# Order of TensorE's products in three attention layers: whole-array products together, scores next to shift, the output product a step later, the output bias on GpSimd

## The chip, the cores and the metric

The kernel runs on one core of a Trainium2 chip. The metric is the time of one execution in device microseconds; the median of several runs is compared. Five engines work side by side: TensorE (PE; its weight loads are shown as PEld), VectorE (DVE), ScalarE (ACT), GpSimd (POOL) and SyncE (SP), which starts transfers. Each takes its own instructions in order and waits for semaphores that others raise. TensorE writes to PSUM, in eight banks; VectorE and ScalarE read it from there.

## The reference

Eight blocks follow each other on x of 16 sequences, 128 tokens, 256 channels. Four are attention blocks on a context, each followed by a feed-forward block. The change touches the attention of the second, third and fourth pair, which compute this (the second with a window, the fourth with rotary embeddings):

```python
q = (Q @ Wq.T + bq).reshape(B, Lq, H, DH).transpose(0, 2, 1, 3)
k = (K @ Wk.T + bk).reshape(B, Lk, H, DH).transpose(0, 2, 1, 3)
v = (V @ Wv.T + bv).reshape(B, Lk, H, DH).transpose(0, 2, 1, 3)
scores = jnp.einsum('bhlp,bhmp->bhlm', q, k) / math.sqrt(DH)
attn = jax.nn.softmax(scores, axis=-1)
out = jnp.einsum('bhlm,bhmp->bhlp', attn, v)
out = out.transpose(0, 2, 1, 3).reshape(B, Lq, D)
return out @ Wo.T + bo          # x = x + this, of layernorm(x) and the context
```

There are 16 heads of 16 channels.

## The kernel before

`attention(nc, env, layer, windowed, rotary)` is called three times: windowed (layer 1), full (layer 2), rotary (layer 3). It holds all 16 sequences in SBUF. A first stage projects keys, values and queries and turns the normalised x (`xn`, made by VectorE, in the rotary layer by ScalarE). Then a loop of steps follows, one sequence n entering at each, with the work on a sequence spread over several steps. Every engine has its own copy of the loop, and the order within a step is written out by hand: the order in which TensorE's, ScalarE's and VectorE's queues hold their instructions.

The stages of sequence n, in order of the data:

- `maxima(n)` on TensorE: f16 products of all heads, 16 instructions on 32-row tiles of the array; in the windowed layer `add_window` precedes it with eight 64x64 products (line 812). VectorE's `maxima(n, 0)` and `(n, 1)` (line 1149) reduce them, half each, to `neg_max`, of which there is one buffer: they wait for `max_turned`, that `turn_maxima(n - 1)` has read it.
- `turn_maxima(n)` (line 838): one whole-array transpose of `neg_max`; ScalarE's `maxima_out(n)` (line 1010) copies it to `neg_maxT`.
- `scores(n)` (line 851): f32 products on 32-row tiles; they wait for ScalarE's exponentials of n - 1 and for the first reduction of n + 1, whose banks they overwrite. `shift(n)` (line 862) adds `neg_maxT` in the same banks.
- ScalarE's `exponentials(n, 0)` and `(n, 1)` (line 1016). The products of `maxima(n + 2)` wait for the first of them.
- `weigh_values(n)` (line 874): 32 products on 32-column tiles, after both exponentials and after `normalise(n - 1)` has read the bank; ScalarE's `sums_out(n)` (line 1028) copies the result.
- `turn_sums(n)` (line 881): four whole-array transposes; VectorE's `normalise(n)` (lines 1155 and 1158): reciprocal and product, to `att`.
- `turn_attended(n)` (line 888): two whole-array transposes; ScalarE's `attended_out(n)` (line 1023).
- `output(n)` (line 895): four whole-array products; VectorE's `add_output(n)` (line 1164) adds them to X, `restate(n)` (line 100) takes the statistics of X for the next block.

`add_bias(n)` on VectorE (line 1102) adds the output bias to X. `hold_clock` (line 55) gives TensorE whole-array products whose result nobody reads. `normal_ahead` is a chain of small VectorE instructions that prepares the next block's normalisation from the statistics of the first 12 sequences.

TensorE's step n before is: turn_maxima(n), maxima(n + 1), turn_sums(n - 2), output(n - 3), scores(n), turn_attended(n - 2), shift(n), weigh_values(n - 1). VectorE's step n: maxima(n + 1, 0), add_bias(n), normalise(n - 2), add_output(n - 3), maxima(n + 1, 1), restate(n - 3).

## Time and profile before

| | us |
|---|---|
| median of 3 runs (2058.22 to 2061.71) | 2058.24 |
| the profiled execution | 2056.44 |
| its span in the trace | 2054.1 |
| PE busy in the span | 1817.9 (88%) |
| DVE busy | 1519.5 (74%) |
| ACT busy | 1133.2 (55%) |
| POOL busy | 158.7 (8%) |

How to read the rows below. A row of the timeline has the start in us from the start of the span, the time from the first start to the last end in us, the engine, the line of the kernel, the operation, the tile written and the tiles read, their shapes, how many instructions are merged in it, and in square brackets how long the engine stood idle before it and what ended that. Ends of matmuls are modelled. A row of the view of one line has the engine, the operation, the count, the least, median and greatest duration in ns, and the first and last start in us. A row of the windows table has the stretch, its length, then for PE, PEld, DVE, ACT and POOL the busy time with the number of instructions, the granted clock of TensorE as a share of full speed, the share of DMA, and GB/s.

### The profile page before, as it was taken

How to read it: one execution, taken by the hardware profiler on the slowest of the kernel's cores; microseconds unless marked ns; L12 is line 12 of the kernel's file. 1: busy time of each engine (PE TensorE's matmuls, PEld its weight loads, DVE VectorE, ACT ScalarE, POOL GpSimd, SP SyncE). 2: the span in 40 equal slices, each digit the busy share in tenths (PEclk: the TensorE clock that was granted, in tenths of full speed). 3: DMA queues.
4: the chain of work that ended last, by engine and by line, in shares of the span. 5: the costliest groups of instructions: out<-in, count | busy, mean ns of one | idle time of the engine just before them, and what ended most of it. 6: DMA issues, size and time to landing. Idle time of an engine off the chain costs nothing. (4 is left out here: it accounts for less than half of the span.)

```text
span 2054.1 us, 40735 instructions
## 1 busy us (share of the span) xinstructions
PE 1817.9 (88%) x16084; PEld 1324.4 (64%) x16084; DVE 1519.5 (74%) x3172; ACT 1133.2 (55%) x1916; POOL 158.7 (8%) x129
## 2 busy tenths in 40 slices
PE   7959258997799999999999999988997897799994
PEld 6844155665466666666666666655674466688884
DVE  6987886667777777777777776787766777688886
ACT  3535754556366666666666665526542654467762
POOL 0001300000000000000000000000000100244431
PEclk9979689998999999999999999999999998799997
DMA  6120001003000000000000000010001001577775
GB/s 222 47 79 0 0 1 52 2 3 114 21 22 22 22 21 22 22 22 22 23 24 24 15 1 1 1 53 2 3 21 56 1 3 46 187 255 245 248 258 173
DMA packets 80365, 120.90 MB, mean 59 GB/s; under 512 B 9840, under 2 KB 62512, under 8 KB 80048
## 3 DMA queue, kind: packets, MB, share of 16 engines
q1 hardware_dynamic: 75760, 106.22, 15.6%
q0 software_dynamic: 4416, 12.06, 1.7%
q8 instruction: 130, 2.13, 0.4%
q14 instruction: 59, 0.48, 0.1%
HBM read 103.58 MB, written 14.68 MB: 58 GB/s over the span
## 5 line engine op out<-in xcount | busy, mean ns | idle before, releaser
L2586 PE MATMUL sl_ps_eo<-sl_w,sl_hT 128*128 128x256 f16 x3072 | 353.2, 273 | 0.8 <-DVE sl_hT L2829 0.7
L2563 PE MATMUL sl_ps_h<-sl_slot_inT,sl_w 128*128 128x512 f16 x1536 | 338.3, 379 | 0.5 <-ACT sl_h L2706 0.5
L2586 PEld LDWEIGHTS sl_ps_eo<-sl_w,sl_hT 128*128 128x128 f16 x3072 | 298.5, 98 | 35.8 <-DVE sl_hT L2829 1.3
L2706 ACT ACTIVATE sl_h<-sl_ps_h,sl_b1T 128x512 f32<-128x512 f32 x256 | 175.6, 687 | 170.3 <-PE sl_ps_h L2563 163.3
L2563 PEld LDWEIGHTS sl_ps_h<-sl_slot_inT,sl_w 128*128 128x128 f16 x1536 | 149.9, 98 | 176.3 <-ACT sl_h L2706 2.4
L2829 DVE TENSOR_TENSOR sl_hT<-sl_h,sl_hT 128x512 f16<-128x512 f32 x256 | 176.8, 692 | 102.2 <-ACT sl_hT L2709 97.9
L1149 DVE TENSOR_REDUCE at_neg_max<-at_ps 128x8 bf16<-128x1024 f32 x96 | 116.9, 1220 | 68.2 <-PE at_ps L831 68.2
L2125 PE MATMUL mo_ps_h<-mo_xgT,mo_w 128*128 128x256 f16 x1104 | 125.9, 275 | 3.5 <-issue 2.1
L2843 DVE SCALAR_TENSOR_TENSOR sl_result<-sl_ps_eo,sl_b 128x256 f32<-128x256 f32 x128 | 54.3, 424 | 97.8 <-PE sl_ps_eo L2586 93.5
L2136 PE MATMUL mo_ps_eo<-mo_w,mo_hT 128*128 128x256 f16 x1104 | 124.1, 273 | 0.0
L2125 PEld LDWEIGHTS mo_ps_h<-mo_xgT,mo_w 128*128 128x128 f16 x1104 | 108.1, 99 | 19.0 <-issue 5.8
L2136 PEld LDWEIGHTS mo_ps_eo<-mo_w,mo_hT 128*128 128x128 f16 x1104 | 107.1, 98 | 12.0
L1016 ACT ACTIVATE at_probT<-at_ps 128x1024 f32<-128x1024 f32 x96 | 98.6, 1027 | 15.0 <-PE at_ps L862 15.0
L2188 ACT ACTIVATE mo_h<-mo_ps_h,mo_b 128x256 f32<-128x256 f32 x184 | 77.0, 475 | 46.6 <-issue 42.8
L1224 POOL MEMSET at_v<- 128x2048 f32 x6 | 10.7, 1816 | 1122.5 <-POOLq L85 1122.5
L2709 ACT ACTIVATE sl_hT<-sl_h 128x512 f16<-128x512 f32 x128 | 80.6, 629 | 4.0
L1023 ACT ACTIVATE at_attT<-at_ps 128x256 f32<-128x256 f32 x48 | 18.4, 383 | 109.9 <-PE at_ps L888 109.9
L2685 ACT ACTIVATE sl_combT<-sl_ps_lt 128x512 f32<-128x512 f32 x32 | 19.1, 597 | 108.5 <-PE sl_ps_lt L2542 108.5
L1615 PE MATMUL qf_ps<-qf_xqT,qf_w_inT 128*128 128x512 f16 x288 | 66.5, 393 | 8.3 <-DVE qf_xqT L1814 6.0
L2317 DVE SCALAR_TENSOR_TENSOR mo_w<-mo_w_raw,mo_w 128x1024 f16<-128x1024 f32 x46 | 56.2, 1223 | 23.9 <-ACT mo_w L2170 23.9
L2208 POOL DMA_INDIRECT mo_xg<-x_rows,mo_from_i x46 | 60.7, 1320 | 146.3 <-DVE mo_from_i L2299 131.3
L2170 ACT ACTIVATE mo_w<-mo_w_raw 128x1024 f16<-128x1024 f32 x46 | 48.5, 1056 | 38.9 <-DMA mo_w_raw<-in_L_ffn_W 38.9
(435 smaller groups left out, 3629.8 us busy)
## 6 DMA issues: line engine op xcount, KB each, us to landing
mo_w_raw<-in_L_ffn_W SPq DMA_DIRECT2D x46, 1024.0 KB, 8.7
sl_w_in<-in_L_ffn_w SPq DMA_DIRECT2D x16, 1024.0 KB, 5.4
at_ctxT<-ctx_pairs SPq DMA_DIRECT2D x9, 512.0 KB, 7.3
mo_w_raw<-pair_rows SPq DMA_DIRECT2D x4, 1024.0 KB, 9.0
mo_b<-in_L_ffn_b SPq DMA_DIRECT2D x23, 128.0 KB, 4.9
ac_attention_w<-L_attention_w SPq DMA_DIRECT2D x3, 768.0 KB, 12.4
w_pairs<-ac_w_pair SPq DMA_DIRECT2D x3, 768.0 KB, 3.2
ac_ctx_all<-in_ctx SPq DMA_DIRECT2D x4, 512.0 KB, 8.2
```

The costliest lines, as they stand in the source:

```text
L1016: act.activation(probT[:, n % 2, 2 * pair:2 * pair + 2].rearrange("p r j q -> p r (j q)"), ps[:, at:at + 2], ACT.Exp, scale=SCALE).then_in ...
L1149: dve.tensor_reduce(neg_max[:, 2 * pair:2 * pair + 2, 0:HR], ps[:, at:at + 2].rearrange("p r (j k) -> p r j k", j=HR), AX.X, ALU.max, nega ...
L1615: last = pe.matmul(pair(q)[:, g], w_inT[:, w, i, k, c * P:(c + 1) * P], xqT[:, x, k, tokens], start=(k, a) == (0, 0), stop=(k, a) == (C - ...
L2125: last = pe.matmul(ps_h[:, q % 3, j % 2], w1_of(m, wp)[:, k, j * P:(j + 1) * P], xgT[:, m % 2, xp, k], start=(k, a) == (0, 0), stop=(k, a) ...
L2136: last = pe.matmul(ps_eo[:, s, 0:D], hT[:, m % 2, hp, j, s * P:(s + 1) * P], w2_of(m, wp)[:, j], start=(j, a) == (0, 0), stop=(j, a) == (H ...
L2188: act.activation(h[:, q % 2, j % 2], ps_h[:, q % 3, j % 2], ACT.Relu, bias=b1[:, m % WB, j:j + 1], scale=1.0 / W_SCALE).then_inc(h_ready, 1)
L2208: pool.indirect_dma_start(xg[:, m % XB, s], None, env.x_rows, bass.IndirectOffsetOnAxis(ap=from_i[:, q:q + 1].bitcast(U32), axis=0)).then_ ...
L2563: last = pe.matmul(ps_h[:, j % 2], w1[:, e % 2, w, k, j * P:(j + 1) * P], slot_inT[:, q % 2, x, k].rearrange("p b s -> p (b s)"), start=(k ...
L2586: last = pe.matmul(ps_eo[:, b % 2, 0:D], hT[:, hp, j, b * P:(b + 1) * P], w2[:, e % 2, w, j], start=(j, a) == (0, 0), stop=(j, a) == (HJ - ...
L2706: act.activation(h[:, j % 2], ps_h[:, j % 2], ACT.Gelu, bias=b1T[:, q // G4, j:j + 1], scale=1.0 / W_SCALE).then_inc(h_ready, 1)
L2709: act.activation(hT[:, 0, j], h[:, j % 2], ACT.Copy).then_inc(h_high, 1)
L2829: dve.tensor_tensor(hT[:, 1, j], h[:, j % 2], hT[:, 0, j], ALU.subtract).then_inc(h_split, 1)
```

## The change

TensorE's step n becomes: weigh_values(n - 2), maxima(n + 1), turn_attended(n - 3), turn_sums(n - 2), turn_maxima(n), output(n - 4), scores(n), shift(n); turn_maxima(0) stands ahead of the loop, and there is one more step. VectorE does both reductions first, then normalise(n - 2), add_output(n - 4) and restate(n - 4); normal_ahead comes a step later. ScalarE's loop is put in the order that fits. The transposed maxima move from bank 7 to columns of bank 6 that nobody reads between the turned sums, and the waits for who uses which bank are changed with it. The bias additions move from VectorE's steps to GpSimd, each as soon as `xn` of its sequence is made; in the rotary layer they stand ahead of GpSimd's casts.

```diff
+UNREAD = DH + 4
...
-        ps_max = ps_a[:, 0, 0:P // 2].bitcast(BF16)
+        ps_max = ps[:, 6].bitcast(BF16).rearrange("p (k i) -> p k i", i=2 * 32)[:, :, 2 * UNREAD:2 * UNREAD + P // H]
...
             def turn_maxima(n):
                 pe.wait_ge(max_ready, 2 * n + 2)
-                enough(pe, attT_ready, n - 2)
...
                 enough(pe, att_ready, n)
+                pe.wait_ge(maxT_ready, min(n + 2, B))
...
             def turn_attended(n):
                 pe.wait_ge(att_ready, n + 1)
-                enough(pe, out_added, n)
+                enough(pe, attT_ready, n)
+                enough(pe, out_added, n - 1)
...
             def output(n):
                 pe.wait_ge(attT_ready, n + 1)
-                pe.wait_ge(maxT_ready, min(n + 4, B))
+                enough(pe, out_added, n)
...
-            for n in range(B + 3):
-                if n < B:
-                    turn_maxima(n)
-                if n == 1:
-                    hold_clock(pe, env, ps[:, 6, 0:P], 2)
+            turn_maxima(0)
+            for n in range(B + 4):
+                if 2 <= n < B + 2:
+                    weigh_values(n - 2)
                 if n + 1 < B:
                     maxima(n + 1)
+                if n < 3:
+                    hold_clock(pe, env, ps[:, 7, 0:P], 4)
+                if 3 <= n < B + 3:
+                    turn_attended(n - 3)
                 if 2 <= n < B + 2:
                     turn_sums(n - 2)
-                if n >= 3:
-                    output(n - 3)
-                if n < 2:
-                    hold_clock(pe, env, ps[:, 6, 0:P], 4)
+                if 1 <= n < B:
+                    turn_maxima(n)
+                if n >= 4:
+                    output(n - 4)
                 if n < B:
                     scores(n)
-                if 2 <= n < B + 2:
-                    turn_attended(n - 2)
-                if n < B:
                     shift(n)
-                if 1 <= n <= B:
-                    weigh_values(n - 1)
...
-            for n in range(B + 2):
-                if n >= 2:
-                    attended_out(n - 2)
+            for n in range(1, B + 3):
+                if n <= B:
+                    exponentials(n - 1, 0)
+                if 2 <= n < B + 2:
+                    sums_out(n - 2)
+                if n <= B:
+                    exponentials(n - 1, 1)
                 if n < B:
-                    exponentials(n, 0)
-                if 1 <= n <= B:
-                    sums_out(n - 1)
-                if n + 1 < B:
-                    maxima_out(n + 1)
-                if n < B:
-                    exponentials(n, 1)
+                    maxima_out(n)
+                if n >= 3:
+                    attended_out(n - 3)
...
             def normalise(n):
                 link = Links(dve, att_link, 1, n)
                 dve.wait_ge(sums_turned, n + 1)
+                dve.wait_ge(maxT_ready, min(n + 3, B))
...
             def add_output(n):
                 dve.wait_ge(out_made, n + 1)
+                dve.wait_ge(attT_ready, min(n + 2, B))
...
-            for n in range(B + 3):
+            for n in range(B + 4):
                 if n + 1 < B:
                     maxima(n + 1, 0)
-                if n < B:
-                    add_bias(n)
+                    maxima(n + 1, 1)
                 if 2 <= n < B + 2:
                     normalise(n - 2)
-                if n >= 3:
-                    add_output(n - 3)
-                if n + 1 < B:
-                    maxima(n + 1, 1)
-                if n == AHEAD + 3:
+                if n >= 4:
+                    add_output(n - 4)
+                if n == AHEAD + 4:
                     normal_ahead(dve, t, env, 1, restated, AHEAD, rows_only=windowed)
-                if n >= 3:
-                    restate(n - 3)
+                if n >= 4:
+                    restate(n - 4)
...
+            pool.wait_ge(consts_in, CONSTS)
+            for n in range(B):
+                pool.wait_ge(t.xn_ready, n + 1)
+                pool.tensor_tensor(t.X[:, n], t.X[:, n], bo[:], ALU.add).then_inc(bo_added, 1)
```

## Rows read from the trace of the kernel before

**Rows 1.** Windows table: most steps of the rotary layer; the full layer's tail.
```profile
1634.00:1706.00 72.00, 68.45 (x1271) 47.45 (x1270) 54.52 (x108) 42.41 (x69) 0.00 (x0) 1.00 0.01 3
...
1480.00:1492.00 12.00, 8.71 (x120) 6.10 (x112) 6.83 (x31) 4.25 (x7) 0.00 (x0) 1.00 0.00 0
```

**Rows 2.** Timeline of the rotary layer, one step, from scores to scores.
```profile
1664.18 0.25 DVE L1155 RECIPROCAL at_inv_sum<-at_ps 128x16 f32<-128x16 f32 x1
...
1664.21 1.15 PE L851 MATMUL at_ps<-at_QT,at_KT 32*128 32x256 f32 x16
1664.46 0.42 DVE L1158 TENSOR_TENSOR at_att<-at_ps,at_inv_sum 128x256 f32<-128x256 f32 x1
1664.81 0.41 DVE L1164 TENSOR_TENSOR X<-X,at_ps 128x256 f32<-128x256 f32 x1
...
1665.36 0.41 PE L888 MATMUL at_ps<-early_ident,at_att 128*128 128x128 f32 x2
...
1665.70 0.40 PE L862 MATMUL at_ps<-at_neg_maxT,at_slot_sel 32*128 32x128 bf16 x16
...
1666.04 1.08 PE L874 MATMUL at_ps<-at_probT,at_v 128*32 128x128 f32 x32
1666.16 1.02 ACT L1016 ACTIVATE at_probT<-at_ps 128x1024 f32<-128x1024 f32 x1
...
1667.05 0.23 PE L838 MATMUL at_ps<-at_ident_b,at_neg_max 128*128 128x128 bf16 x1
...
1667.83 0.42 PEld L881 LDWEIGHTS at_ps<-early_ident,at_sumsT 128*128 128x128 f32 x4 [0.28 <-ACT at_sumsT L1028]
...
1668.33 1.03 PE L895 MATMUL at_ps<-at_wo,at_attT 128*128 128x256 f32 x4
...
1669.29 1.15 PE L851 MATMUL at_ps<-at_QT,at_KT 32*128 32x256 f32 x16
```

**Rows 3.** Timeline of the windowed layer, its first two steps.
```profile
367.63 1.02 ACT L1016 ACTIVATE at_probT<-at_ps 128x1024 f32<-128x1024 f32 x1 [2.57 <-PE at_ps L862]
...
368.80 0.62 PE L812 MATMUL at_ps<-at_window_b,at_ident_b 64*64 64x256 bf16 x8 [0.55 <-ACT at_probT L1016]
...
369.81 1.22 DVE L1149 TENSOR_REDUCE at_neg_max<-at_ps 128x8 bf16<-128x1024 f32 x1 [2.74 <-PE at_ps L831]
...
371.18 0.62 PE L812 MATMUL at_ps<-at_window_b,at_ident_b 64*64 64x256 bf16 x8 [0.34 <-DVE at_neg_max L1149]
...
371.74 1.15 PE L851 MATMUL at_ps<-at_QT,at_KT 32*128 32x256 f32 x16
...
373.03 1.08 PE L874 MATMUL at_ps<-at_probT,at_v 128*32 128x128 f32 x32
```

**Rows 4.** Timeline of the windowed layer, a later step: maxima, then turn_sums.
```profile
404.90 0.40 PE L831 MATMUL at_ps<-at_ctxT,at_QT_half 32*128 32x128 f16 x16
...
405.23 0.66 PE L881 MATMUL at_ps<-early_ident,at_sumsT 128*128 128x128 f32 x4
```

**Rows 5.** View of line 862 (shift): the windowed layer, then the rotary layer.
```profile
L862 PE MATMUL at_ps<-at_neg_maxT,at_slot_sel x256: 214/214/225, 367.2 to 456.5; 32*128 32x128 bf16 x128
...
L862 PE MATMUL at_ps<-at_neg_maxT,at_slot_sel x256: 214/214/226, 1631.1 to 1706.4; 32*128 32x128 bf16 x128
```

**Rows 6.** Timeline of VectorE at the windowed layer's end: normal_ahead to statistics; last statistics.
```profile
454.79 0.90 DVE L143 BATCH_NORM_AGGREGATE ahead_meanvar<-stats 128x2 f32<-128x6 f32 x12
...
458.39 0.43 DVE L100 BATCH_NORM_STATS2 stats<-X 128x6 f32<-128x256 f32 x1
...
467.37 0.43 DVE L100 BATCH_NORM_STATS2 stats<-X 128x6 f32<-128x256 f32 x1
```

**Rows 7.** Timeline of the rotary layer's projections: a GpSimd cast beside VectorE.
```profile
1607.84 1.04 POOL L1229 CAST at_QT_half<-at_QT 128x1024 f16<-128x1024 f32 x1 [50.64 <-ACT at_QT L987]
1607.86 1.56 DVE L1118 TENSOR_TENSOR at_q_turned<-at_by_cos,at_by_sin 128x512 f32<-128x512 f32 x1
```

**Rows 8.** View of line 1110: by_sin, whose one input is in PSUM.
```profile
L1110 DVE TENSOR_TENSOR at_by_sin<-at_ps,at_sinT x16: 678/682/691, 1563.8 to 1624.2; 128x512 f32<-128x512 f32 x16
```

More of the change, by code:

```diff
@@ L1009, in maxima_out @@
                 enough(act, shifted, n)
-                act.activation(neg_maxT[:], ps_max, ACT.Copy).then_inc(maxT_ready, 1)
+                act.activation(neg_maxT[:].rearrange("p (k i) -> p k i", i=P // H), ps_max, ACT.Copy).then_inc(maxT_ready, 1)
             def exponentials(n, pair):
@@ L1099, in normal_x @@
                                   ALU.subtract, ALU.mult).then_inc(t.xn_ready, 1)
-            def add_bias(n):
-                dve.tensor_tensor(t.X[:, n], t.X[:, n], bo[:], ALU.add).then_inc(bo_added, 1)
             def rope(job, to, wait_for, ready):
```

## Prediction

> **What bounds the kernel now.** The change touches only the three attention layers, so I read the windows table first: in the 72 us that hold most steps of the rotary layer TensorE is busy 68.45 us at a granted clock of 1.00 (the 2.4 GHz level), VectorE 54.52 and ScalarE 42.41 [rows 1]. A step is a TensorE queue that hardly stops. The timeline of one rotary step shows its links; from the scores of one step to those of the next are 5.08 us [rows 2]. The gaps of TensorE are turns between array shapes. The scores, with turn_attended between them and shift, reach weigh_values after 1.83 us [rows 2]; where the first steps have no turn_attended, the same stretch takes 1.29 [rows 3]. That half microsecond is what the new order goes for. Nothing else of the three layers is slack in this sense: VectorE spends two reductions of 1.22 [rows 3], a reciprocal, a product, an addition and the statistics on each step, which fit beside TensorE only because the first reduction may start early.
>
> I take links as distances between starts. An instruction's consumer on another engine starts 0.06 after its written end (shift 1665.70 + 0.40, exponential 1666.16 [rows 2]), and one that follows on the same VectorE starts 0.07 before it (attended product to addition, 0.35 for 0.42 [rows 2]).
>
> **What the change removes, on TensorE alone.** Scores and shift together: 1.83 becomes 1.29, minus 0.54. turn_maxima loses its own turn of shapes and turn_attended too, but both stay as work: four whole-array transposes take 0.49 to 0.50 from turn_sums to output [rows 2], so 0.12 each, and 0.24 for the two of turn_attended. A step of TensorE's own pieces in the new order would be: scores to weigh_values 1.29, weigh_values to the next shape 1.01 (to turn_maxima [rows 2]), maxima 0.33 [rows 4], attended 0.24, sums 0.49, maxima's transpose 0.12, output 0.96 [rows 2]: 4.44 against 5.08. The rule behind this is in the Trainium skill, TensorEngine Tiling (Array Packing), section Key Properties: changing the tiling mode, not just the tile, drains TensorE. The trace agrees (1.83 against 1.29); by that rule alone the three layers would gain, which is the first rival below.
>
> **What the new order ties together.** neg_max has one buffer, so VectorE's maxima(n + 1) waits until turn_maxima(n) has read it; this wait is not touched by the diff. Before, turn_maxima(n) opened step n, ahead of the products of maxima(n + 1), and the wait was long over. Now it stands behind maxima(n + 1), turn_attended(n - 3) and turn_sums(n - 2), and turn_sums waits for ScalarE's sums_out, which waits for weigh_values. Behind the waiting reduction stand, on VectorE, the second reduction, normalise(n - 2), add_output and restate; and weigh_values(n - 1) waits for normalise(n - 2). That closes a loop through three engines, which I walk for the layers without a window:
> weigh_values to turn_sums 1.79, ended by ScalarE's copy (1666.04 to 1667.83 [rows 2]; the products of maxima and turn_attended, 1.01 + 0.33 + 0.24 = 1.58, are hidden in it); turn_sums to turn_maxima 0.49; its end and the reaction 0.23 + 0.06 = 0.29; two reductions at 1.22 - 0.07 = 1.15, 2.30, both now ahead of normalise; reciprocal to product 0.28; product to weigh_values 0.55, as from add_output to turn_attended (1664.81 to 1665.36 [rows 2]). Sum 5.70 against 5.08.
> Scores in this loop: they wait for the first reduction, 1.37 after its start [rows 3], so they start 1.79 + 0.49 + 0.29 + 1.37 = 3.94 behind weigh_values, 0.95 later shift, and weigh_values follows at 5.70, not at 5.23: normalise comes last.
>
> In the windowed layer the window's products (0.56 from their start to the scores [rows 3]; taken as the same ahead of maxima) come twice a step, and another loop is longer. From turn_maxima: 0.29 to the reduction, 1.37 to the window's products of the scores, 0.56 to the scores. The next maxima have to wait for the first exponential: scores to shift 1.29 - 0.34 = 0.95, shift to exponential 0.46, exponential to the window's products 1.17 (367.63 to 368.80 [rows 3]), 2.58 together, more than the 1.29 + 1.01 that TensorE needs; before, turn_maxima stood in this place. Then 0.56 to maxima, 0.33, 0.24, 0.49 to turn_maxima. Sum 6.42. The VectorE loop is shorter here: 1.01 + 0.56 + 0.33 + 0.24 + 0.49 + 0.29 + 2.30 + 0.28 + 0.55 = 6.05.
>
> **Sum of the steps.** From shift(0) to shift(15) there are 15 distances. The first two have the four clock-holding products in them (eight whole-array instructions at 0.12, 0.97). Without a window: exponential 0.46, maxima 1.17 later, 0.33, 0.97, 0.29, 1.37, 0.95: 5.54; the next with turn_sums 0.49 more, 6.03; twelve of 5.70, 68.4; the last has no reduction to wait for: 0.81 (5.70 - 3.94 - 0.95) + 1.79 + 0.49 + 0.12 + 0.96 + 0.95 = 5.12. Total 85.1. The trace has 1706.4 - 1631.1 - 0.2 = 75.1 in the rotary layer (the row's last start is the last of one shift's sixteen products, so 0.2 comes off) [rows 5], and the full layer repeats its pattern, so twice +10.0. With the window: 6.66 + 7.15 + 12 x 6.42 + 5.2 = 96.0 against 456.5 - 367.2 - 0.2 = 89.1 [rows 5], +6.9.
>
> **The end of a layer.** There is one more step, but the tail's links (attended, output, addition) are those of before. What moves is normal_ahead: it now stands in step 16 ahead of normalise(15), 3.6 us of VectorE (454.79 to 458.39 [rows 6]) in a tail of 467.37 - 456.3 = 11 us, where it used to lie a step before normalise(14) and was over when turn_sums(14) came. Bounds: nothing, if the chain outlasts it, and the whole 3.6. Counted from shift(15), turn_sums(14) comes at 0.34 + 1.79 = 2.13, weigh_values(15) at 2.13 + 0.71 + 0.28 + 0.55 = 3.67 and turn_sums(15) at 5.46, so normalise(15) could begin at 6.2. VectorE's addition behind output(12) ends at some 4.4, and with 3.6 and the statistics it is free at 8.4. I take 2.0 for each layer, 6.0.
>
> **Edits costed at nothing, and their cover.** add_bias leaves VectorE: 16 additions a layer that lay in VectorE's waits; it would help only if the reductions did not wait. weigh_values' wait for maxima_out is for the step before. normalise's wait for maxima_out(n) is covered by two reductions, 2.3 us, in which ScalarE ends at most one exponential (1.02 [rows 3]) and a short copy. add_output's wait for attended_out has output's 1 us before it and the reductions beside it. Scores keep their waits. SP has no new DMA. Without these covers each would cost its own copy, under 0.4.
>
> **GpSimd's additions.** The trace has no such instruction of GpSimd; they run in the projections, as each xn is ready, and ahead of the rotary layer's casts in its queue. What they can do is seen beside those casts: a 1.04 us cast started at 1607.84, and the VectorE product of two SBUF tiles at 1607.86 took 1.56 instead of 0.69 [rows 7]; by_sin, with one input in PSUM, stayed between 678 and 691 ns in all 16 [rows 8]. In the other two layers VectorE has no instruction with two SBUF tiles between the first xn and the last, so the lower bound there is zero; none reaches below zero but what add_bias gave back, already counted. In the rotary layer at most one such instruction falls into a group of four: 4 x 0.87 = 3.5. I take zero, nearest to the by_sin row, and keep 3.5 for the range. The Trainium skill, SBUF — State Buffer, section Who interferes with whom, says that a VectorE instruction with two SBUF inputs contends with a GpSimd instruction that reads SBUF and that whoever is second is blocked. The 1.56 agrees; the sum is the same by it.
>
> **Result.** 10.0 + 10.0 + 6.9 + 6.0 = 32.9. The profiled execution took 2056.44 (span 2054.1), so 2089.3; the median of the three runs, 2058.24, is 0.1% above it, and there it is 2091. Error of the walk: the links not seen in this order are product to weigh_values (0.49 to 0.66), turn_sums to turn_maxima (0.39 to 0.55), attended to sums (0.12 to 0.34) and weigh_values to the next shape (0.9 to 1.1): about -0.25 and +0.3 for each of 36 steady steps, -9 and +11. With the tail (-6 to +5) not all one way, 2077 to 2106.
>
> **Rivals.**
> 1. Faster: the shapes decide, as the rule on draining would have it. The place is the start of the first reduction: if it followed the products of maxima and not turn_maxima, the loop would fall below TensorE's own sum. It decides once the reduction starts 0.62 earlier than in my walk without a window, 0.42 with it. Without the wait a step is 2.58 + 0.33 + 0.24 + 0.49 + 0.12 + 0.96 = 4.72 and with the window 5.84; over 30 and 15 steps minus 13, plus 6 for the tails: 2051. For it: the 0.54. Against it: one buffer, and a reduction would overwrite what is still to be read.
> 2. No change: the loops close, but my links are too long by half a microsecond each step, as if the transposes came with less than half of their cost and turn_sums did not wait: 2055 to 2062.
> 3. Slower still by the clock: TensorE waits twice a step and its granted clock falls to the lower level (1.2 GHz) in half of the 24 steady steps of two layers; its part of the loop, 1.01 + 0.49, doubles: +18, 2109. Against it: the full layer's tail, with TensorE busy 8.71 of 12 us, kept 1.00 [rows 1].
> 4. Slower still by GpSimd: its additions hold up 16 instructions of VectorE in every layer by a part of the 0.87, +15, 2106. For it: 1.56. Against it: by_sin.
>
> **How the numbers follow.** Forecast 0.78, rival 1 0.07, rival 2 0.05, rival 3 0.05, rival 4 0.05. The range 2075 to 2108 takes the walk's errors, the 3.5 and most of rival 4, and leaves rivals 1 to 3 and some of the forecast's edge out. Measurement tells 0.2%, some 4 us. Faster 0.07, same 0.05, slower 0.88.
>
> **What would show it.** The first reduction starts 0.3 behind turn_maxima in every steady step and is released by it, not by maxima; two reductions stand back to back and normalise behind them; weigh_values, in the layers without a window, waits for attended (DVE); steps of 5.7 and 6.4; scores to weigh_values 1.29. The granted clock stays at 1.00 there. I am wrong if the reductions start right behind maxima, or if the loss is seen in the projections.

## The result and the profile after

| | before | after |
|---|---|---|
| median, us | 2058.23 (4 runs, 2054.48 to 2061.71) | 2107.72 (4 runs, 2104.63 to 2112.19) |
| ratio, 95% interval | | 1.0245 [1.0222, 1.0268] |
| profiled execution; its span | 2056.44; 2054.1 | 2105.77; 2104.0 |

The changed kernel is 49.5 us slower. Slower was forecast, but 16.7 us less of it (2091.0). Busy time and instructions on the pages of the kernel before and then of the kernel after:

```profile
PE 1817.9 (88%) x16084; PEld 1324.4 (64%) x16084; DVE 1519.5 (74%) x3172; ACT 1133.2 (55%) x1916; POOL 158.7 (8%) x129
```

```profile
PE 1826.1 (87%) x16096; PEld 1342.4 (64%) x16096; DVE 1515.7 (72%) x3124; ACT 1136.8 (54%) x1916; POOL 194.9 (9%) x177
```

TensorE has 16096 instructions for 16084 (four more, of hold_clock, in each of the three layers) and is busy 8 us longer, in a span 50 us longer: what was added is waiting, not work. Where it lies is told by cutting each of the three layers at the same marks: from GpSimd's memset of v to turn_maxima(0) ("projections"), from shift(0) to shift(15) ("steps"), from shift(15) to the start of the last statistics ("tail"). All are distances between starts in the timelines, in us. The first two rows are the kernels before and after; the others are the experiments that follow, and all but e7 start from the kernel after.

| kernel | windowed: projections / steps / tail | full | rotary | span |
|---|---|---|---|---|
| before | 43.88 / 89.16 / 11.02 | 42.68 / 75.28 / 11.03 | 73.36 / 75.20 / 11.03 | 2054.1 |
| after | 48.00 / 96.27 / 14.63 | 46.23 / 84.95 / 14.43 | 75.04 / 85.93 / 15.57 | 2104.0 |
| e1_two_max: two buffers | 45.45 / 85.67 / 14.38 | 46.42 / 70.47 / 14.42 | 75.75 / 70.42 / 14.43 | 2064.0 |
| e6_norm_mid: normalise between the reductions | 46.10 / 96.40 / 14.63 | 46.58 / 84.19 / 14.94 | 73.53 / 80.14 / 14.51 | 2092.9 |
| e7_before_pool: before, with GpSimd's additions | 45.66 / 89.17 / 11.03 | 46.67 / 75.06 / 11.03 | 76.15 / 74.97 / 11.04 | 2067.1 |
| e2_dve_bias: additions on VectorE | 43.86 / 96.25 / 14.45 | 42.84 / 86.16 / 15.52 | 74.87 / 89.14 / 14.88 | 2105.0 |
| e3_late_pool: GpSimd's additions late | 43.78 / 96.26 / 14.95 | 42.70 / 86.17 / 13.48 | 72.93 / 88.84 / 14.55 | 2099.1 |
| e10_hold: e3 with hold_clock in each step | 44.07 / 95.42 / 14.69 | 42.71 / 85.30 / 15.10 | 76.62 / 86.73 / 14.61 | 2099.4 |
| e4_ahead: normal_ahead a step earlier | 46.82 / 96.26 / 12.93 | 46.51 / 86.17 / 13.27 | 75.63 / 88.84 / 13.62 | 2102.9 |
| e5_all: e1, e3 and e4 together | 44.81 / 85.68 / 12.93 | 42.80 / 70.47 / 13.27 | 76.74 / 72.13 / 14.15 | 2051.3 |
| e9_drain: e5 with the last outputs earlier | 43.91 / 85.68 / 12.54 | 42.68 / 70.47 / 12.88 | 73.36 / 71.85 / 12.89 | 2053.8 |
| e11_drain_late: e9 with output(13) behind weigh_values(15) | 44.15 / 85.68 / 11.90 | 42.96 / 70.48 / 12.25 | 73.21 / 72.14 / 12.24 | 2049.1 |

Of the 49.9 us between the two spans, the steps have 7.11 + 9.67 + 10.73 = 27.5 (forecast 26.9), the tails 3.61 + 3.40 + 4.54 = 11.55 (6.0), the projections 4.12 + 3.55 + 1.68 = 9.35 (0); 1.5 lie elsewhere.

Each row is one execution, and executions differ: outside the three stretches, where the kernels do nearly the same work, the spans lie between 3.1 us less and 6.1 us more than in the kernel before, and the rotary layer's projections without GpSimd's additions take 72.93 to 76.74. A few us in one row count where other rows repeat them. The steps and tails do; of the projections the windowed layer (45.45 to 48.00 with the additions beside xn, 43.78 to 44.81 without) and the full layer (46.23 to 46.67, 42.68 to 42.96), but not the rotary layer's 1.68.

**Steps.** The view of line 862 (shift) of the kernel after, in the windowed, the full and the rotary layer, against [rows 5] (count, least, median and greatest ns, first and last start):

```profile
L862 PE MATMUL at_ps<-at_neg_maxT,at_slot_sel x256: 214/214/214, 370.5 to 467.0; 32*128 32x128 bf16 x128
...
L862 PE MATMUL at_ps<-at_neg_maxT,at_slot_sel x256: 214/214/215, 1423.8 to 1508.9; 32*128 32x128 bf16 x128
...
L862 PE MATMUL at_ps<-at_neg_maxT,at_slot_sel x256: 214/214/309, 1666.2 to 1752.3; 32*128 32x128 bf16 x128
```

96.5, 85.1 and 86.1 us, where [rows 5] has 89.3 and 75.3. Twelve steps of the full layer take 5.69 each, twelve of the windowed layer 6.43. One of them, in the timeline of the full layer of the kernel after (to be read against [rows 2]):

```profile
1455.86 2.35 DVE L1146 TENSOR_REDUCE at_neg_max<-at_ps 128x8 bf16<-128x1024 f32 x2 [1.92 <-PE at_ps L838]
...
1457.23 1.15 PE L851 MATMUL at_ps<-at_QT,at_KT 32*128 32x256 f32 x16 [0.56 <-DVE at_neg_max L1146]
...
1458.13 0.25 DVE L1153 RECIPROCAL at_inv_sum<-at_ps 128x16 f32<-128x16 f32 x1
...
1458.41 0.42 DVE L1156 TENSOR_TENSOR at_att<-at_ps,at_inv_sum 128x256 f32<-128x256 f32 x1
...
1458.94 1.08 PE L875 MATMUL at_ps<-at_probT,at_v 128*32 128x128 f32 x32 [0.34 <-issue]
...
1460.72 0.66 PE L882 MATMUL at_ps<-early_ident,at_sumsT 128*128 128x128 f32 x4
...
1461.22 0.22 PE L838 MATMUL at_ps<-at_ident_b,at_neg_max 128*128 128x128 bf16 x1
...
1461.54 1.22 DVE L1146 TENSOR_REDUCE at_neg_max<-at_ps 128x8 bf16<-128x1024 f32 x1 [1.92 <-PE at_ps L838]
```

VectorE stands 1.92 us before the reduction, until line 838 (turn_maxima) has read neg_max, and both reductions run before the reciprocal. The links are 2.27 to the reciprocal, 0.28, 0.53, 1.78, 0.50 and 0.32: 5.68 from reduction to reduction. The view names no releaser for weigh_values (its 0.34 is put down to issue); it starts 0.11 behind the end of the attended product, 1458.41 + 0.42. In the kernel before, the reduction waited for the products of maxima (line 831) and never for turn_maxima:

```profile
1657.63 1.23 DVE L1149 TENSOR_REDUCE at_neg_max<-at_ps 128x8 bf16<-128x1024 f32 x1 [1.10 <-PE at_ps L831]
```

**Projections.** The view of line 1098 (VectorE makes xn, once for each sequence of the windowed and the full layer), first before, then after:

```profile
L1098 DVE TENSOR_SCALAR at_xn_ring<-X,at_meanvar,at_rstd x32: 398/403/411, 325.1 to 1384.8; 128x256 f32<-128x256 f32 x32
```

```profile
L1098 DVE TENSOR_SCALAR at_xn_ring<-X,at_meanvar,at_rstd x32: 402/694/729, 324.3 to 1401.7; 128x256 f32<-128x256 f32 x32
```

The median instruction went from 403 to 694 ns (446 in another execution of the same code, e1: how many meet an addition differs). The timeline of the windowed layer's projections of the kernel after shows what runs beside it, and what follows on TensorE:

```profile
345.04 0.72 POOL L1224 TENSOR_TENSOR X<-X,at_bo 128x256 f32<-128x256 f32 x1 [0.23 <-DVE at_xn_ring L1098]
345.21 0.69 DVE L1098 TENSOR_SCALAR at_xn_ring<-X,at_meanvar,at_rstd 128x256 f32<-128x256 f32 x1
...
347.34 1.47 PE L795 MATMUL at_ps<-at_wT,at_ctxT 128*128 128x256 f16 x12 [2.57 <-DVE at_v L1126]
...
348.64 1.85 PE L803 MATMUL at_ps<-early_ident,at_xn_ring 128*128 128x128 f32 x8
```

GpSimd starts adding the bias as soon as one xn is done, and the next xn falls beside it. TensorE waits 2.57 us for the v that VectorE makes behind these xn, where it waited 1.67 before, and the eight transposes that follow take 1.85 instead of 1.04. The same two rows before:

```profile
346.46 1.47 PE L794 MATMUL at_ps<-at_wT,at_ctxT 128*128 128x256 f16 x12 [1.67 <-DVE at_v L1129]
347.76 1.04 PE L802 MATMUL at_ps<-early_ident,at_xn_ring 128*128 128x128 f32 x8
```

The windows table says why the transposes are longer; before (343 to 364), then after (PE, PEld, DVE, ACT and POOL busy, then the granted clock):

```profile
343.00:364.00 21.00, 17.10 (x130) 9.88 (x131) 15.73 (x31) 13.69 (x26) 0.00 (x0) 1.00 0.01 2
```

```profile
343.00:366.56 23.56, 19.10 (x116) 10.48 (x113) 16.22 (x31) 13.61 (x24) 2.90 (x4) 0.86 0.00 1
...
1420.00:1450.00 30.00, 21.38 (x441) 16.81 (x442) 15.85 (x21) 15.24 (x23) 0.00 (x0) 1.00 0.01 2
1660.00:1690.00 30.00, 21.19 (x369) 16.67 (x372) 13.37 (x15) 14.06 (x22) 2.44 (x2) 0.89 0.01 2
1752.00:1769.00 17.00, 12.05 (x124) 8.56 (x115) 8.17 (x38) 4.28 (x7) 0.00 (x0) 0.80 0.00 1
```

A part of the stretch ran at 1.2 GHz after that wait. So the 4.12 us are two things: e1 and e7, whose clock is 1.00 from 318 to 366 us, lose 1.57 and 1.78 in this layer's projections, and the rest came with the lower clock. In the rotary layer, of VectorE's products of two SBUF tiles beside the additions, one took 1.21 us (from 1598.37); the others kept their 0.69 to 0.71. The other rows are the first steps of the full layer, still at 1.00, those of the rotary layer, and its tail, 0.80.

**Tails.** The windowed layer's tail of the kernel after, against [rows 6]:

```profile
471.35 0.90 DVE L143 BATCH_NORM_AGGREGATE ahead_meanvar<-stats 128x2 f32<-128x6 f32 x12
...
472.23 0.66 PE L882 MATMUL at_ps<-early_ident,at_sumsT 128*128 128x128 f32 x4 [0.23 <-ACT at_sumsT L1028]
...
475.31 0.24 DVE L1153 RECIPROCAL at_inv_sum<-at_ps 128x16 f32<-128x16 f32 x1
...
476.48 0.41 PE L890 MATMUL at_ps<-early_ident,at_att 128*128 128x128 f32 x2 [2.73 <-DVE X L1163]
476.73 1.03 PE L897 MATMUL at_ps<-at_wo,at_attT 128*128 128x256 f32 x4
...
478.89 2.04 PE L897 MATMUL at_ps<-at_wo,at_attT 128*128 128x256 f32 x4 [1.14 <-DVE X L1163]
```

The last sums are turned at 472.23 + 0.66 = 472.89, but the reciprocal starts at 475.31, when normal_ahead (from 471.35) and the statistics behind it are through, 2.42 later. Counted from shift(15), that is 8.51 for 7.09 before: the last sums are turned 1.0 earlier than before and then wait. From this reciprocal to the last statistics 6.12 us pass for 3.93. Two outputs are still to come in them (476.73 and 478.89), the last at the lower clock level, 2.04 for 1.03.

### The profile page after: what moved, and what is told of

Same layout as the page of the kernel before. It is cut to its first block and busy times, and to the rows that moved or that the text cites. A ratio compares the mean times of both kernels' runs of the same rounds, so it can differ in the third digit from the quotient of the medians.

```text
span 2104.0 us, 40770 instructions
## 1 busy us (share of the span) xinstructions
PE 1826.1 (87%) x16096; PEld 1342.4 (64%) x16096; DVE 1515.7 (72%) x3124; ACT 1136.8 (54%) x1916; POOL 194.9 (9%) x177
## 5 line engine op out<-in xcount | busy, mean ns | idle before, releaser
L851 PE MATMUL at_ps<-at_QT,at_KT 32*128 32x256 f32 x768 | 56.4, 406 | 21.8 <-DVE at_neg_max L1146 21.8
```

## Experiments on the steps

My theory of the steps is the loop through the one neg_max. The rival: the new order itself costs the time.

**Two buffers for neg_max**, so that the reduction of n + 1 doesn't wait for turn_maxima(n):

```diff
-        neg_max = t.sb("neg_max", [P, R, 32], BF16)
+        neg_max = t.sb("neg_max", [P, 2, R, 32], BF16)
...
-                enough(dve, max_turned, n)
+                enough(dve, max_turned, n - 1)
...
```

> The changed kernel with two buffers for neg_max, so that a reduction waits for the transpose before last; nothing else differs. Theory (the single buffer ties the reductions to turn_maxima, and so the loop through three engines): the first reduction starts right behind the products of maxima, steps fall from 5.69 to about 4.7 in the two layers without a window and from 6.43 to about 5.8 in the windowed one; over some 15 steps a layer this is 36 us less than the changed kernel, about 2072 us. Rival (the order of TensorE's products itself, its drains and ScalarE's exponentials set the step): steps stay at 5.7 and 6.4, about 2107 us.

2068.59 us (2065.97 to 2069.63), ratio 1.0044 [1.0028, 1.0061]: 39 us come back. Its windowed layer's timeline:

```profile
412.38 0.40 PE L832 MATMUL at_ps<-at_ctxT,at_QT_half 32*128 32x128 f16 x16
...
412.84 2.35 DVE L1146 TENSOR_REDUCE at_neg_max<-at_ps 128x8 bf16<-128x1024 f32 x2 [2.03 <-PE at_ps L832]
...
413.43 0.22 PE L838 MATMUL at_ps<-at_ident_b,at_neg_max 128*128 128x128 bf16 x1
```

The reduction starts behind the products of maxima (line 832), 0.59 ahead of turn_maxima. All three layers' steps are then shorter than before the change: 85.67, 70.47 and 70.42 against 89.16, 75.28 and 75.20. The new order is a gain once the buffer is doubled; the loop had turned it into a loss. A second buffer in the old order was not run, but there no reduction waits for turn_maxima (the row of the kernel before, above), and the additions' move alone gives 0.2 (e7). Which part of the gain is the turns between shapes was not separated.

**normalise put back between the two reductions**, one buffer. The walk has two loops: without a window normalise is in it, with the window it isn't.

```diff
                 if n + 1 < B:
                     maxima(n + 1, 0)
-                    maxima(n + 1, 1)
                 if 2 <= n < B + 2:
                     normalise(n - 2)
+                if n + 1 < B:
+                    maxima(n + 1, 1)
```

> The changed kernel with normalise(n - 2) back between the two reductions; one buffer for neg_max as in the changed kernel. Theory (two different loops set the step: without a window the one through both reductions, normalise and weigh_values, with it the one through the first reduction and the scores): without a window one reduction of 1.15 us leaves the loop, which falls to 4.55, and the loop through the scores is then longest, 0.29 + 1.37 + 2.58 + 0.33 + 0.24 + 0.49 = 5.3; the windowed layer stays at 6.43. Some 10 us less, 2097 us. Rival (one loop, through normalise, everywhere): the windowed layer falls too, by up to 0.4 a step; or (normalise is not in any loop) nothing moves.

2097.95 us (two runs, 2094.78 and 2101.11), ratio 1.0184 [1.0166, 1.0202]. Steps without a window are 5.32, windowed ones stay at 6.43. In its full layer the reciprocal comes 1.14 behind the first reduction, where the kernel after has 2.27, and the loop closes in 5.32 through the scores and the exponential that the next maxima wait for (the full layer's 84.19 in the table has two first steps of 7.91 and 7.76 in it; the granted clock was 0.80 from 1415 to 1450 us):

```profile
1458.69 1.22 DVE L1146 TENSOR_REDUCE at_neg_max<-at_ps 128x8 bf16<-128x1024 f32 x1 [1.55 <-PE at_ps L838]
...
1459.83 0.25 DVE L1153 RECIPROCAL at_inv_sum<-at_ps 128x16 f32<-128x16 f32 x1
...
1461.36 1.08 PE L875 MATMUL at_ps<-at_probT,at_v 128*32 128x128 f32 x32
...
1462.63 0.41 PE L832 MATMUL at_ps<-at_ctxT,at_QT_half 32*128 32x128 f16 x16 [0.20 <-ACT at_probT L1016]
...
1464.01 1.23 DVE L1146 TENSOR_REDUCE at_neg_max<-at_ps 128x8 bf16<-128x1024 f32 x1 [1.55 <-PE at_ps L838]
```

## Experiments on GpSimd's additions and the clock

**The kernel before with GpSimd's additions alone:**

```diff
-                if n < B:
-                    add_bias(n)
...
+            for n in range(B):
+                pool.wait_ge(t.xn_ready, n + 1)
+                pool.tensor_tensor(t.X[:, n], t.X[:, n], bo[:], ALU.add).then_inc(bo_added, 1)
```

> The kernel before with one part of the change alone: the bias additions on GpSimd as each xn is ready, none on VectorE. Theory (GpSimd's additions hold up normal_x): projections longer by about 4, 3.6 and 1.7 us, 2068 us, normal_x at 0.7 us beside an addition. Rival (the loss in the projections came with the changed steps): 2059 us.

2063.08 us (10 runs), ratio 1.0019 [1.0008, 1.0031]. By medians the part costs 3.3 us; in the profiled execution, one of its longer ones (2068.91), the projections are 1.78, 3.99 and 2.79 longer, and another 4.9 of its span lies outside the three stretches. VectorE got 0.2 of it back in the steps of each layer without a window. The view of its line 1098:

```profile
L1098 DVE TENSOR_SCALAR at_xn_ring<-X,at_meanvar,at_rstd x32: 403/479/822, 327.3 to 1393.1; 128x256 f32<-128x256 f32 x32
```

So it's the additions, and not the new order, that lengthen xn.

**The changed kernel without them beside xn**: additions back on VectorE behind restate, or on GpSimd behind the casts and turn_maxima(0).

```diff
...
+                if n < B:
+                    add_bias(n)
...
-            for n in range(B):
-                pool.wait_ge(t.xn_ready, n + 1)
-                pool.tensor_tensor(t.X[:, n], t.X[:, n], bo[:], ALU.add).then_inc(bo_added, 1)
```

> The changed kernel with the bias additions back on VectorE, at the end of its step, behind restate. Theory (GpSimd's additions hold up VectorE's normal_x, and TensorE waits behind that): normal_x back to 0.40 us, the projections shorter by 4.1, 3.6 and 1.7 us, steps unchanged because VectorE waits in each of them anyway; about 2098 us. Rival 1 (the projections are longer for another reason, the transfers or the phase of the clock): unchanged, 2107 us. Rival 2 (VectorE is the bound of the steps): steps 0.34 us longer each, 2114 us.

```diff
-            pool.wait_ge(consts_in, CONSTS)
-            for n in range(B):
-                pool.wait_ge(t.xn_ready, n + 1)
-                pool.tensor_tensor(t.X[:, n], t.X[:, n], bo[:], ALU.add).then_inc(bo_added, 1)
             if rotary:
...
+            pool.wait_ge(consts_in, CONSTS)
+            pool.wait_ge(t.xn_ready, B)
+            pool.wait_ge(max_turned, 1)
+            for n in range(B):
+                pool.tensor_tensor(t.X[:, n], t.X[:, n], bo[:], ALU.add).then_inc(bo_added, 1)
```

> The changed kernel with GpSimd's 16 additions begun only when the first maxima are turned, in the rotary layer behind its casts. Theory (what counts is that they meet normal_x): projections as in the kernel before, additions beside reductions that read PSUM cost nothing, about 2098 us. Rival (GpSimd's additions hold up VectorE wherever they run): the first three or so steps of each layer become longer by up to 0.3 us for each addition, about 2105 us.

2106.84 us (1.0229 [1.0212, 1.0246]) and 2107.58 us (1.0242 [1.0220, 1.0265]). Both totals missed, though the projections of the first two layers did what was expected: 43.86 and 42.84, 43.78 and 42.70, as before the change, with xn at 0.40 again. A part was given back in the steps of the other two layers, 86.17 and 88.84 in the second kernel, 4.1 us more than in the kernel after. That execution's span is still 4.9 shorter; by medians nothing is left, and the longer executions were not profiled. The second kernel's windows, the projections and then the first steps of the full and the rotary layer:

```profile
346.00:365.36 19.36, 15.46 (x108) 8.56 (x105) 14.29 (x28) 12.35 (x21) 0.00 (x0) 1.00 0.01 1
1420.00:1450.00 30.00, 22.83 (x440) 18.01 (x444) 15.51 (x22) 14.27 (x23) 7.44 (x11) 0.94 0.01 2
1660.00:1690.00 30.00, 23.20 (x387) 17.89 (x387) 12.96 (x17) 13.32 (x22) 6.04 (x9) 0.82 0.01 2
```

The clock is 1.00 in the projections, but 0.94 and 0.82 in the steps, where the kernel after has 1.00 and 0.89; single steps of 6.1 to 7.9 us stand there among those of 5.69. Is the clock the reason, or GpSimd's additions beside the steps (they aren't in the first of the two kernels, nor in e4 below, and both lost as much there)?

**The second kernel, with two products of hold_clock ahead of each step's scores**, where TensorE waits for the reduction; their result is read by nobody.

```diff
                 enough(pe, prob_ready, 2 * n)
+                if n > 0:
+                    hold_clock(pe, env, ps[:, first, 0:P], 2)
```

> The changed kernel with GpSimd's additions begun only when the first maxima are turned, and with two clock-holding products (four whole-array instructions, 0.49 us) ahead of every step's scores, where TensorE waits 0.56 us for the first reduction. Theory (with the additions out of the way the projections are as before, but TensorE's pauses in the first steps let its granted clock fall to the lower level in stretches that cost 1 to 4 us a layer, and this hid the gain): no lower clock in the steps, 85.0 us from shift(0) to shift(15) in both layers without a window, projections 43.9, 42.7 and 73, total 2095 to 2099 us with less scatter. Rival (the pauses have nothing to do with it, the added products only lengthen the loop): the lower stretches stay, or steps become longer, 2107 us or more.

2099.08 us (2094.49 to 2101.23), ratio 1.0185 [1.0161, 1.0210]: by medians 8.5 below the second kernel (2100.84 to 2113.94, its profiled execution the shortest), with more work on TensorE. The steps of its profile are 95.42, 85.30 and 86.73 for 96.26, 86.17 and 88.84, 3.8 us less; 0.8 of it is in the windowed layer, where no step of the second kernel was at the lower level, so that part isn't the clock's. Its windows of the two layers:

```profile
1415.00:1450.00 35.00, 28.75 (x541) 22.82 (x538) 18.79 (x26) 18.21 (x28) 11.39 (x16) 1.00 0.01 2
1660.00:1690.00 30.00, 25.19 (x439) 20.00 (x431) 12.96 (x17) 13.91 (x22) 8.61 (x13) 0.89 0.01 2
```

GpSimd is busy there as before, so it isn't its additions. In the full layer no step is left at the lower level, in the rotary layer one. The loop leaves TensorE waits in every step, and some were followed by 1.2 GHz: in the second kernel's profile that took back about 4 of the 7.8 us that the projections of the first two layers had won. That it took the rest too in the longer executions is likely by the medians, not shown. Why a given stretch fell and another didn't, these runs don't settle.

## Experiments on the tail

**normal_ahead a step earlier**, behind restate:

```diff
-                if n == AHEAD + 4:
-                    normal_ahead(dve, t, env, 1, restated, AHEAD, rows_only=windowed)
                 if n >= 4:
                     restate(n - 4)
+                if n == AHEAD + 3:
+                    normal_ahead(dve, t, env, 1, restated, AHEAD, rows_only=windowed)
```

> The changed kernel with normal_ahead one step earlier, behind restate(11) in step 15, and so ahead of normalise(14) and not of normalise(15). Theory (in the tail VectorE's chain holds up normalise(15), turn_attended(15) and what follows): the tails shorter by about 1.5 us each, 2103 us. Rival (the tail is longer by its links, output waiting for addition, and by the clock): unchanged within 1 us, 2107 us.

The tails lose 1.70, 1.16 and 1.95, 4.8 us in all; the total, 2109.0 (2101.02 to 2113.94, ratio 1.0241 [1.0208, 1.0274]), doesn't show it beside steps that were slower at the lower clock. The end of its windowed tail:

```profile
477.37 0.41 PE L890 MATMUL at_ps<-early_ident,at_att 128*128 128x128 f32 x2 [1.14 <-DVE X L1163]
477.62 1.03 PE L897 MATMUL at_ps<-at_wo,at_attT 128*128 128x256 f32 x4
479.79 1.10 PE L897 MATMUL at_ps<-at_wo,at_attT 128*128 128x256 f32 x4 [1.14 <-DVE X L1163]
```

Against the same rows of the kernel after, turn_attended(15) comes 0.76 earlier behind shift(15) (8.92 for 9.68), and from there to the last output's end 3.52 pass instead of 4.45, since that output now takes 1.10 and not 2.04. The same sums in the other layers are 0.22 and 0.94, 0.34 and 1.61. So of the 4.8 1.3 come from an earlier turn_attended(15), and 3.5 from outputs that were at the lower clock. That clock came after the longer wait of TensorE, 2.73 for 1.14; that the wait is its cause is argued from this order alone, and in the next kernel's rotary layer the last output took 1.98 behind a wait of 1.14.

Nor is 1.3 the whole price of normal_ahead, which now holds up another instruction. normalise(14), for which weigh_values(15) waits, starts right behind it, 3.65 behind shift(15), where in the kernel after it starts 2.82 behind it (first row below: the kernel after; second: this kernel; shift(15) at 466.80 and 468.45):

```profile
469.62 0.26 DVE L1153 RECIPROCAL at_inv_sum<-at_ps 128x16 f32<-128x16 f32 x1 [2.83 <-PE at_ps L882]
```

```profile
472.10 0.26 DVE L1153 RECIPROCAL at_inv_sum<-at_ps 128x16 f32<-128x16 f32 x1
```

In the other two layers it is 4.00 for 2.82. The kernel before has 2.82 too.

Besides that delay, two outputs are left, 2.17 apart, both behind turn_attended(15), where the order before had one: an output a step later is a round more of product and addition at the end.

**All three together** (two buffers, additions late, normal_ahead early):

> The changed kernel with two buffers for neg_max, GpSimd's additions only once the first maxima are turned, and normal_ahead behind restate(11). Theory (three separate causes, the single buffer, the additions beside normal_x, normal_ahead in the tail; the new order of TensorE's products is itself a gain): from the 2068.6 us of the two buffers alone the projections give back some 8 and the tails some 4.5, so 2056 us, below the kernel before by 0.15%. Rival (the three share the same loss, or the granted clock takes back what they give, as it did where each was undone alone): 2062 us or more.

2056.4 us (12 runs, 2047.12 to 2064.89), ratio 0.9984 [0.9968, 1.0000]. Undoing the three takes back the whole loss. Against the two buffers alone the median is 12.2 us less (12.5 expected): that is what the additions beside xn and the place of normal_ahead cost together, with the lower clock that followed them. In its profile the steps of the three layers are 11.4 us less than before, the tails 7.3 more, the projections 4.4 more (in the next kernel, which has the same projections, nothing more).

**That kernel with the last outputs earlier**: output(13) ahead of weigh_values(15), output(14) ahead of turn_attended(15), add_output(13) ahead of normalise(15).

```diff
+                if n == B + 1:
+                    output(n - 4)
                 if 2 <= n < B + 2:
                     weigh_values(n - 2)
                 if n + 1 < B:
                     maxima(n + 1)
+                if n == B + 2:
+                    output(n - 4)
...
-                if n >= 4:
+                if n >= 4 and n not in (B + 1, B + 2):
                     output(n - 4)
...
+                if n == B + 1:
+                    add_output(n - 4)
                 if 2 <= n < B + 2:
                     normalise(n - 2)
-                if n >= 4:
+                if n >= 4 and n != B + 1:
                     add_output(n - 4)
```

> As the kernel with all three undone, and in the last three steps output stands ahead: output(13) ahead of weigh_values(15), output(14) ahead of turn_attended(15), and add_output(13) ahead of normalise(15). Theory (the tail of the changed kernel is longer by one round of output and addition, about 2.2 us, because output is a step later): tails shorter by 1.3 to 2.2 us each, some 5 us less than with the three undone, 2051 us. Rival (the tail hangs on normalise and the copies): unchanged.

2054.18 us (7 runs), ratio 0.9964 [0.9950, 0.9977]. The tails gave only 0.39 in each of the first two layers: in the full layer's tail output(13) itself waits, and weigh_values(15) behind it.

```profile
1482.83 1.10 PE L897 MATMUL at_ps<-at_wo,at_attT 128*128 128x256 f32 x4 [1.53 <-DVE X L1167]
1483.86 1.08 PE L875 MATMUL at_ps<-at_probT,at_v 128*32 128x128 f32 x32
```

**output(13) behind weigh_values(15) instead:**

```diff
-                if n == B + 1:
-                    output(n - 4)
                 if 2 <= n < B + 2:
                     weigh_values(n - 2)
...
-                if n == B + 2:
+                if n in (B + 1, B + 2):
                     output(n - 4)
```

> The same edits as in the kernel that reordered the last steps, but the output product of sequence 13 stands behind weigh_values(15), not ahead of it, where it had waited 1.53 us for the addition of sequence 12 while weigh_values(15) stood behind it (weigh_values(15) started at 1483.86; normalise(14), which it needs, was over at 1482.35). Theory: the part of the longer tail that was left (12.5 to 12.9 us from the last shift to the last statistics against 11.0 before the change) is the one more round of output and addition that the later output brings. With the two spare rounds placed where TensorE only waits for ScalarE, weigh_values(15) starts about 1482.4, the last output about 1487.0 instead of 1488.93, and the tails come to 10.7 to 11.2 in all three layers; total 2048 to 2051. Rival: the round is not what is left, something else ends last in the tail (the copy of the attended values, the reciprocal, normal_ahead); the tails stay within 0.3 of 12.5 to 12.9, and the total at 2054.

2052.19 us (12 runs), ratio 0.9971 [0.9957, 0.9984]; the two kernels can't be told apart by their times. The tails are 11.90, 12.25 and 12.24, another 0.64 less, between the theory's 11 and the rival's 12.5. In its full layer:

```profile
1485.24 0.38 PE L890 MATMUL at_ps<-early_ident,at_att 128*128 128x128 f32 x2
1485.66 0.38 ACT L1025 ACTIVATE at_attT<-at_ps 128x256 f32<-128x256 f32 x1 [2.01 <-PE at_ps L890]
1486.13 0.42 DVE L1165 TENSOR_TENSOR X<-X,at_ps 128x256 f32<-128x256 f32 x1 [1.02 <-PE at_ps L897]
...
1486.70 1.10 PE L897 MATMUL at_ps<-at_wo,at_attT 128*128 128x256 f32 x4 [1.08 <-DVE X L1165]
```

By the two reorderings 1.03 and 1.02 us of the round are shown (windowed and full layer, against the kernel with all three). The addition of 14 still runs behind the copy of 15 (the change's new wait in add_output) and the last output behind that addition; this link was not tried further. 0.88, 1.22 and 1.21 us of the tails are left over those before. normalise(14) starts 0.83, 1.19 and 1.18 later behind shift(15) than before, since normal_ahead still stands ahead of it; the sizes agree, but no run puts normal_ahead behind normalise(14), so that this is what is left is not shown. Both kernels beat the one before by 0.3 to 0.4%.

## Why the prediction was right, and where it was wrong

- **The loop of the steps: right in mechanism and size.** 5.69 for 5.70, 6.43 for 6.42; first steps of the full layer 5.57 and 6.04 for 5.54 and 6.03; 27.5 us for 26.9. The two-buffer kernel showed the cause, the kernel with normalise in the middle the two loops. One line of what would show it was at odds with the walk itself: scores to weigh_values is 1.71 without a window (1457.23 to 1458.94), near the 1.76 that 5.70 - 3.94 gives, not 1.29. Another, the clock at 1.00, held in the full layer's steps and not in the rotary layer's first ones (0.89).
- **GpSimd's additions at zero: wrong, the first term that failed.** The step was that no instruction of VectorE between the first and the last xn has two SBUF tiles, so the bound was zero. The xn instruction itself, with one tile, grew from 403 to 694 ns. Looking for one shape of instruction left out the one beside which additions run. The loss was seen in the projections, which the prediction had named as a sign of being wrong. Its size is less sure than that it is there: 9.35 in the profile of the kernel after, with the lower clock in it and 1.68 of the rotary layer that is within the scatter; 3.3 by medians on the kernel before. The 3.5 kept for the rotary layer was for products of two SBUF tiles; one of them became longer there, by 0.5. The same section of the Trainium skill that I drew on (SBUF — State Buffer, Who interferes with whom) also names tensor_scalar among the VectorE operations that can use both ports and then contend with GpSimd. The rows agree that they contend (0.69 us beside an addition, 0.40 alone); I hadn't applied that part.
- **The tail: wrong, the second term.** "The tail's links are those of before" was the step that failed. What the walk saw is there: VectorE free at 8.4 and the last sums at 6.2 behind shift(15), measured 8.51 and 6.09. But it took their difference as the loss, without the kernel before, where normalise(15) starts at 7.09; so its 6.0 stand for 3.9 (1.42, 1.22 and 1.21). The other 7.7 of the 11.55 lie behind normalise(15): the last outputs ran at the lower clock (3.5, which came back when normal_ahead stood a step earlier), and an output a step later means one more round behind the last attended values (the other 4.2 in three layers; the last two outputs start 2.17 apart, and moving outputs recovered 1.0 in each of the first two layers).
- **The rivals.** That the shapes decide and the change gains was out, by the wait on which it hung; with two buffers its steps (4.7 and 5.80) are near its 4.72 and 5.84. That kernel's shorter steps agree with the rule on draining (TensorEngine Tiling (Array Packing), Key Properties, in the Trainium skill), though no run separates the turns between shapes from the rest of the order. The slower cases by GpSimd and by the clock were each part of it: the additions not through two-tile instructions, and the clock not in half of the steps but after the longer waits of the projections, in some first steps and in the last outputs. I set the clock aside because a tail with TensorE busy 8.71 of 12 us held 1.00 [rows 1]; the rotary layer's first steps, busy 21.19 of 30, didn't.
- **The range** ended at 2108, and that 2107.72 is just inside it is luck: GpSimd's additions and the clock, each kept as an alternative of small chance, came together, and the one more round in the tail, which it did not have, came on top.

## What to carry to other kernels

When an order moves the reader of a single-buffered value later, follow the writer's wait through every engine until the loop closes, and compare that sum with the busy engine's own; a second buffer can turn the same order from a loss into a gain, as it did here. Before work goes to GpSimd, look at what VectorE runs in exactly that stretch, at each instruction and not at one kind. And when work is put a step later, count the rounds that remain behind the last item, and take a delay against the start that the kernel before really had.

## What was not expected of the hardware

- A VectorE tensor_scalar with one SBUF tile, 128x256 f32, took 0.69 us beside a GpSimd addition of 0.72, and 0.40 alone. It ended 0.14 behind the addition's end (345.90 and 345.76), not a whole 0.40; spans of GpSimd are rough.
- The granted clock in first steps of the same loop was 1.00 in one layer and 0.89 in another, at 21.38 and 21.19 us of TensorE in 30; with GpSimd's additions moved away it was 0.94 and 0.82, and two idle products a step then brought 8.5 us back by medians of four executions each.
